# Rounding the FFN's hidden rows on one engine instead of two, in a fused cross-attention and FFN kernel

## The reference

```python
def quantize_rowwise(x):
    absmax = jnp.max(jnp.abs(x), axis=1, keepdims=True)
    q = jnp.clip(_round_ste(x * (Q / absmax)), -Q, Q)      # Q = 127
    return (q, absmax)
X2_pre = int8_matmul_dequant_bias(X1_q, W1_q.T, sX1, sW1, B1)   # 112 x 2048 per batch
X2 = jax.nn.gelu(X2_pre, approximate=True)
X2_q, sX2 = quantize_rowwise(X2)
out = int8_matmul_dequant_bias(X2_q, W2_q.T, sX2, sW2, B2)
```

## Time and profile before

| | us |
|---|---|
| median of three runs | 771.72 |
| the profiled execution's own time | 769.71 |
| span of that execution, first to last instruction | 767.9 |
| PE busy in the span | 669.3 (87%) |
| VectorE busy | 559.8 (73%) |
| ScalarE busy | 445.3 (58%) |
| GpSimd busy | 293.5 (38%) |

### The profile page before, as it was taken

One profiled execution on the slowest core, in us unless ns is written; L12 is line 12 of the kernel. 1 busy time (PEld: TensorE's weight loads), 2 busy tenths in 40 slices (PEclk: granted clock), 3 DMA queues, 4 the chain that ended last, 5 costly groups with the idle time before them and its releaser, 6 DMA issues.

```text
span 767.9 us, 15796 instructions
## 1 busy us (share of the span) xinstructions
PE 669.3 (87%) x5576; PEld 517.3 (67%) x5576; DVE 559.8 (73%) x1270; ACT 445.3 (58%) x1084; POOL 293.5 (38%) x538
## 2 busy tenths in 40 slices
PE   0366989999999999999999999999999999997744
PEld 0255767777786777777777777786777777774522
DVE  2788675777878696869687777878696868677554
ACT  2312555666666675757666666666675757565501
POOL 1135152524344353535352524344353535231211
PEclk9998898999999999999999999999999999998778
DMA  9526641020302011121111020202011120000000
GB/s 303 222 62 212 225 155 42 4 72 1 86 2 74 14 42 45 33 55 33 55 31 55 3 85 2 83 5 74 14 38 49 35 66 10 25 2 25 1 13 12
DMA packets 24684, 45.38 MB, mean 59 GB/s; under 512 B 2144, under 2 KB 12128, under 8 KB 23984
## 3 DMA queue, kind: packets, MB, share of 16 engines
q1 hardware_dynamic: 24608, 44.38, 18.8%
HBM read 40.70 MB, written 3.67 MB: 58 GB/s over the span
## 4 chain that ended last, share of the span: by engine, by line
PE 78%; ACT 8%; DVE 6%; issue 4%; DMA 2%; POOL 2%; SPq 0%; POOLq 0%; DVEq 0%
PE ps_ring L797 30%; PE ps_t L827 13%; PE ps_ring L879 8%; PE ps_ring L897 7%; PE ps_s L820 7%; PE ps_t L839 6%; ACT L498 3%; PE ps_ring L866 2%; ACT pT L506 2%; PE ps_ring L790 2%; DMA pT<-in_wvT 1%; ACT probs L498 1%; PE ps_ring L886 1%; PE ps_ring L849 1%; ACT k_sb L485 1%
## 5 line engine op out<-in xcount | busy, mean ns | idle before, releaser
L506 ACT ACTIVATE pT<-ps_t 125x336 f32<-125x336 f32 x256 | 115.2, 450 | 169.1 <-PE ps_t L827 163.5
L498 ACT ACTIVATE probs<-probs,neg_max 112x375 f32<-112x375 f32 x256 | 153.2, 601 | 14.7 <-DVE neg_max L634 14.5
L827 PEld LDWEIGHTS ps_t<-ident,probs 112*125 112x125 f32 x768 | 112.8, 192 | 72.1 <-issue 38.2
L827 PE MATMUL ps_t<-ident,probs 112*125 112x112 f32 x768 | 132.8, 282 | 26.4 <-ACT probs L498 15.8
L634 DVE CUSTOM_DVE_ANT_0 probs<-ps_s,mask_in 112x375 f32<-112x375 f32 x256 | 130.6, 544 | 28.5 <-PE ps_s L820 21.4
L422 POOL TENSOR_TENSOR ctx_lo<-ctx_in,ctx_hi 128x376 fp32r<-128x376 f32 x64 | 66.0, 1035 | 90.5 <-ACT ctx_hi L480 90.4
L797 PE MATMUL ps_ring<-ctx_hi,wk_hi 128*128 128x376 f32 x256 | 92.6, 362 | 0.0
L797 PE MATMUL ps_ring<-wv_hi,ctx_hi 128*125 128x512 f32 x192 | 82.2, 428 | 8.3 <-POOL ctx_lo L422 8.3
L797 PE MATMUL ps_ring<-ctx_lo,wk_hi 128*128 128x376 f32 x256 | 86.1, 336 | 0.0
L797 PE MATMUL ps_ring<-ctx_hi,wk_lo 128*128 128x376 f32 x256 | 86.1, 336 | 0.0
L797 PE MATMUL ps_ring<-wv_hi,ctx_lo 128*125 128x512 f32 x192 | 77.6, 404 | 0.0
(11 more groups left out here) (123 smaller groups left out, 1289.4 us busy)
## 6 DMA issues: line engine op xcount, KB each, us to landing
ctx_in<-in_ctxT SPq DMA_DIRECT2D x32, 375.0 KB, 3.6
h<-in_w2T SPq DMA_DIRECT2D x4, 1024.0 KB, 5.4
b_row<-in_w2T SPq DMA_DIRECT2D x4, 1024.0 KB, 5.3
x_in<-in_x SPq DMA_DIRECT2D x16, 224.0 KB, 2.6
xres<-in_x SPq DMA_DIRECT2D x16, 224.0 KB, 2.6
out<-y SPq DMA_DIRECT2D x16, 224.0 KB, 3.6
mask_in<-in_mask SPq DMA_DIRECT2D x16, 164.1 KB, 3.6
w_q<-in_w1T SPq DMA_DIRECT2D x2, 1024.0 KB, 14.8
```

The costliest lines, as they stand in the source:

```text
L498: nc.scalar.activation(probs[:, hd % SP_RING, :], probs[:, hd % SP_RING, :], ACT.Exp, scale=-1.0, bias=neg_max[:, b % 2, hd:hd + 1], accum ...
L506: nc.scalar.activation(pT[0:LR, hd % PT_RING, :], ps_t[0:LR, 0:LC * N], ACT.Copy).then_inc(pT_s, 1)
L827: last = nc.tensor.transpose(ps_t[0:LR, lc * N:(lc + 1) * N], probs[:, hd % SP_RING, lc * LR:(lc + 1) * LR], ident[0:N, 0:N])
```

## The change

GpSimd's unit `h_quant` goes, with its two operations of 1024 columns in each batch. VectorE's pair in `round_rows` now covers all 2048 columns. The two semaphores for the low half go with it, and both `h_T` units of PE wait for the one semaphore that is raised when all 2048 columns are rounded.

```diff
 POOL_UNITS = (
-    ("q", 0, 1), ("split", 0, 2), ("y_quant", 0, -1), ("h_quant", 0, -1), ("split", 1, 2), ("residual", 0, 0), ("split", 2, 2),
+    ("q", 0, 1), ("split", 0, 2), ("y_quant", 0, -1), ("split", 1, 2), ("residual", 0, 0), ("split", 2, 2),
...
-            def h_quant(b, i):
-                wait_for(pool, hT_pe, 2 * b)
-                round_rows(b, h[0:N, F // 2:F], h_r[:], h_q[:, F // 2:F], h_round, h_quant_s, h_r_s)
...
                 wait_for(dve, hT_pe, 2 * b)
-                round_rows(b, h[0:N, 0:F // 2], h_r[:], h_q[:, 0:F // 2], h_round_lo, h_quant_lo, h_r_s)
+                round_rows(b, h[0:N, :], h_r[:], h_q, h_round, h_quant_s, h_r_s)
...
             def h_T(b, i):
-                pe.wait_ge((h_quant_lo, h_quant_s)[i], b + 1)
+                pe.wait_ge(h_quant_s, b + 1)
```

More of the change, by code:

```diff
@@ L270, in xattn_ffn_kernel @@
         h_quant_s = sem("h_quant_s")
-        h_round_lo = sem("h_round_lo")
-        h_quant_lo = sem("h_quant_lo")
         hT_pe = sem("hT_pe")
@@ L457, in _ @@
             units = {"prepare": prepare, "x_norm": x_norm, "split": split_lo, "x_quant": x_quant, "q": q, "residual": residual,
-                     "y_norm": y_norm, "y_quant": y_quant, "h_quant": h_quant}
+                     "y_norm": y_norm, "y_quant": y_quant}
             run(pool, units, POOL_UNITS)
```

## The result

The changed kernel takes **794.26 us** (median of 6 runs, 792.46 to 801.0), the kernel before 772.21 us beside it (6 runs, 771.01 to 772.54). The ratio is 1.031 with a 95% interval of [1.028, 1.034]: slower. The forecast was 782.5 us with a range up to 787.0. The sign and the place were right, the size was half of what came: 10.8 us were forecast, 22.05 lie between the medians.

A forecast was written before the change was run, and what follows sets the result against it. PE's work plus about 1.2 us of waits was taken to bound the slot. 12 x 0.82 + 1.00 + 0.1 = +10.9 us on the 771.72 median gave 782.5 us, range 780 to 785.5, wider 777.5 to 787.

The forecast's parts named there:

- The bound, the deciding wait, the count: PE bounds the slot; its scores L820 wait for head 3's PSUM banks, 0.82 us in twelve slots, 1.00 in one.
- the 0.36 of slack: Before PE's L820: banks of heads 0 to 3 usable at 402.68, wanted at 403.04, so 0.36 us of VectorE lateness is free.
- The cost of columns and the offsets: VectorE's rounding: 1024 more columns add 0.53 us per operation; each shared operation ends a fixed offset after the other engine's.
- The step that failed: VectorE's first rounding operation gets its turn after GpSimd's L448 alone, ending at 397.19; `xn` ends 1.18 us later.
- From `xn` to head 3 VectorE has no gap to lose: VectorE's reduction, scale operations and scores follow one another, so head 3 is released the full 1.18 us later.
- `h_T` covered: PE's transposes of `h_q`: complete at 399.12, wanted at 400.28; 1.16 us of cover, cost 0.
- The slack of 0.18 in the slot of the earlier trace: In one slot head 3 ends at 361.54 and L820 starts at 361.87: slack 0.18, stall 1.00 us.
- Batch 13: Its rounding has no `xn` behind it and VectorE idles 2.36 us before the next score: cost 0.
- The last batch: Rounding alone on the pair, 1.282 + 1.228 + 0.04 us, on PE's path: +0.1 us, between 0 and +0.3.
- Rival 1: VectorE gets the port pair before L448: within 0.1 to 0.2 of 771.7; chance 0.05 in all slots, 0.05 in some.
- Rival 2: Sharing does not matter once GpSimd rounds nothing; VectorE's pair takes 2.5 us against 3.3: 771.8 us; chance 0.06.
- Rival 3: PE's late start also delays ScalarE and next scores, so the whole 1.18 us per slot comes through: 787.0 us; chance 0.08.

The follow-up runs named there:

- the single delay of experiment 2: Kernel before, with one extra 0.69 us VectorE instruction that nothing reads behind `x_quant` in each slot: 771.21 us.
- the 3.86 and 6.22 us cases: Changed kernel plus a GpSimd `tensor_scalar` behind the sum of `y` and `b2`: with constants, 812.57 us; with SBUF scalars and a wait for `h_r`, 816.56 us.
- the three operations of experiment 2: Kernel before, with three extra VectorE instructions (2.15 us in all) that nothing reads behind `x_quant`: 788.71 us.
- experiment 1: Changed kernel, with GpSimd's sum of `y` and `b2`, and all that follows it, waiting until `h` is rounded: 771.90 us.
- its reordered form: Kernel before, with GpSimd's `split` of part 1 put ahead of GpSimd's half of the rounding: 771.67 us.
- the last variant of experiment 3: Changed kernel plus a GpSimd `tensor_scalar` behind the sum of `y` and `b2`, with scalars from SBUF and a wait for `h_r`: 816.56 us.
- both one-sided waits of experiment 4: Changed kernel, with GpSimd's second `split` (794.82 us) or its residual's bias (793.39 us) waiting until VectorE's first rounding operation is over.

## Why the prediction was right in kind and wrong in size

- **The bound, the deciding wait, the count: right.** The chain, L814's new wait for `neg_max`, thirteen slots, the 0.36 of slack (7.66 to 8.16 less 0.14), and the full passing on of what is above it were as forecast.
- **The cost of columns and the offsets: right.** 1.08 for 2048 columns behind GpSimd's end was measured for the 1.07 forecast, 1.16 for 1.14, 0.83 for 0.86, 0.29 for 0.28.
- **The step that failed:** "The first operation starts at 394.87 as before, gets its turn when L448 is over, and ends at 396.66 + 0.53 = 397.19." It did not get its turn there; the `split` passed it. That is 0.94 us: 1.18 + 0.94 = 2.12, the measured lateness of `xn`. I had read from one sequence that the engines "take turns, one whole instruction each", and carried it over to a GpSimd stream of other instructions. The profile before showed only one such stream, so the turn should have had bounds, as the column cost had: one more `split` ahead makes 13 x (1.18 + 0.94 - 0.36) + 0.1 = 23.0 us, 794.7 in all. The range had no such case, and this is why the time fell outside it.
- **"From `xn` to head 3 VectorE has no gap to lose": wrong by 0.12.** `xn` is 2.12 late and head 3 only 2.00, since VectorE had idled about that long ahead of head 0. Thus 1.64 per slot and not 2.12 - 0.36 = 1.76; the single delay of experiment 2 shows the same hidden part.
- **`h_T` covered: right for the time, but the 1.16 us of cover were not there.** The 0.94 took most of it, and L606 stood behind the bias, not the shorter `split` (2.20 us, 1.90 forecast). L606 ends at 409.84 and L880 starts at 409.89. PE did wait for it, some 0.13 us, though the profile marks no idle time there: the 0.05 between the two is what lies between them where it does mark a wait (0.06 and 0.05 in the 3.86 and 6.22 us cases). Two rows of PE before and two after, with the earlier trace rows between:

```profile
399.96 0.48 PE L827 MATMUL ps_t<-ident,probs 112*125 112x112 f32 x3
401.07 0.78 PE L839 MATMUL ps_t<-pT,v_sb 125*32 125x112 f32 x24 [0.24 <-ACT pT L506]
...
409.45 0.48 PE L821 MATMUL ps_t<-ident,probs 112*125 112x112 f32 x3
410.56 0.78 PE L833 MATMUL ps_t<-pT,v_sb 125*32 125x112 f32 x24
```

  From the start of the rounding, L827 stands at 5.09 and L821 at 5.10, L886 at 5.41 and L880 at 5.54, L839 at 6.20 and L833 at 6.21. The 0.13 came out of the 0.24 for which PE had waited there for ScalarE's `pT`, so the slot lost nothing. With more ahead (the 3.86 and 6.22 us cases) the profile shows PE waiting, 0.58 and 1.96.
- **The slack of 0.18 in the slot of the earlier trace rows** made no difference in the changed kernel: PE's gap there is 1.56 like the others, not 0.18 more. With the three operations of experiment 2 it did show, 1.42 against 1.13.
- **Batch 13: right for the waits.** L604 took 2.37 us and L606 1.23, with VectorE idle 1.92 us behind them (2.36 before), and PE's scores start without a gap at 8.00 from the start of the rounding (7.98 before). The slot is 1.38 longer all the same, for no cause that was shown.
- **The last batch: right.** 1.29 and 1.23 us alone on the pair, PE's first transpose 2.61 us behind the start of the rounding (before 2.35), and `down` 5.00 behind it (4.89): +0.11.
- **Rival 1** (VectorE in first) happened in no steady slot. **Rival 2** is what experiment 1 builds by a wait. **Rival 3**, with its whole 1.18 per slot, was wrong as well: the first 0.36 of the lateness at head 3 never came through.

**What stays open.** With the cause of the time shown (one GpSimd instruction more ahead), which boundary a waiting VectorE gets is not. Ahead of the first operation went one instruction in the kernel before, in its reordered form, and where something behind waits for `h_round`; two in the changed kernel, with its half left out, with the `split` waiting for `h_r`, with the bias first, with scalars from SBUF, and with the later ask; three with constants or a tiny operation; five, three or one in a single execution of the last variant of experiment 3. None of these decides by itself: the columns of VectorE's operation, the kind and length of the next instruction (though two went ahead with scalars from SBUF and three with constants), a wait on it that is already met, and a count of free instructions behind. In the changed kernel and in both one-sided waits of experiment 4, four GpSimd instructions lay ahead of VectorE's three turns in all, where I had reckoned three.

## What to carry to other kernels

Where VectorE and GpSimd share the pair, price a VectorE operation by all the GpSimd work that is ready when it asks, not by one instruction: in these runs the low end is one ahead, the high end the whole run of five. If an operation of VectorE is on a tight chain, let the GpSimd instruction that would pass it wait for a semaphore that this operation raises (one wait gave back all 22 us here), and look at VectorE's next operations too: the same wait one or two instructions further on freed the first operation and lost as much at the second (794.82 and 793.39 us); moving GpSimd's own share away only brings its next work forward into the same place. And reckon from the slack of the waiting engine: of 1.18 or of 2.12 us of lateness it takes the first 0.36 to 0.48 away, and all the rest arrives in every slot.

## What the runs showed of the hardware

- A VectorE operation that waits for the pair need not be served at the next boundary between GpSimd's instructions: two to five GpSimd instructions back to back, none of them slowed, passed it. The Trainium skill (SBUF — State Buffer, section "Who interferes with whom") says that the second engine waits until the first's instruction is over. The trace agrees for the single turns of the earlier trace rows; for the changed kernel it is a lower bound, and the measurement (3.25 us, up to 6.22) decides.
- The granted clock sometimes falls behind the new gap. In the kernel of experiment 4 whose second `split` waits, two slots in a row and then three stretches of the second, columns as in the earlier trace rows:

```profile
235.00:277.80 42.80, 40.20 (x350) 31.21 (x351) 33.72 (x77) 27.32 (x67) 16.63 (x32) 1.00 0.13 39
277.80:322.25 44.45, 41.84 (x350) 32.53 (x350) 33.74 (x77) 27.31 (x67) 16.63 (x32) 0.96 0.13 38
...
285.00:287.00 2.00, 1.27 (x11) 0.76 (x12) 1.97 (x7) 1.70 (x6) 0.00 (x0) 0.92 0.32 115
287.00:289.00 2.00, 2.00 (x9) 1.58 (x8) 1.67 (x5) 0.75 (x2) 0.00 (x0) 0.50 0.04 8
289.00:291.00 2.00, 2.00 (x10) 1.32 (x9) 1.75 (x6) 0.88 (x4) 0.00 (x0) 0.73 0.00 0
```

PE had waited 1.56 us until 285.73; from 287 to 289 it works at 0.50, the level of 1.2 GHz, and the slot is 1.65 us longer, all of it PE's busy time (41.84 against 40.20). VectorE, ScalarE and GpSimd do the same work as in the slot before. It struck one slot of thirteen here, one where the `split` waits for `h_r` (44.42 us), four where VectorE asked later (44.4 to 44.5 us each), seven and ten where the first operation took 3.86 and 3.40, and none in the profiled execution of the changed kernel, whose gap is as long. That this is why executions of the changed kernel scatter (792.46 to 801.0, where the kernel before has 771.01 to 772.54) is likely, but the slower executions have no trace, so it is not shown.
